# A two-layer transformer on one core: GpSimd's two-input operations in halves, and the order planned anew

## The reference

```python
x = x + attn0(layernorm(x))    # 16 heads of 16, causal softmax, w_qkv, w_out
x = x + ffn0(layernorm(x))     # a = entmax15(layernorm(x @ proj)), 16 experts
#   h = gelu((x @ Win1 + bias) * (a @ C1) @ Wout1.T); out = (h @ Win2 + bias) * (a @ C2) @ Wout2.T
x = x + attn1(layernorm(x))    # low-rank q, k, v; half of each head rotated by cos and sin
x = x + ffn1(layernorm(x))     # relu(x @ Ws1)^2 @ Ws2, and routed experts where the gate is 1
```

## Time and profile before

| | |
|---|---|
| Median of 3 runs | 2663.76 us (2661.55 to 2675.57) |
| The profiled execution | 2670.14 us, span 2667.7 us |
| TensorE | busy 2407.9 us, 90% |
| VectorE | busy 2035.3 us, 76% |
| ScalarE | busy 1869.8 us, 70% |
| GpSimd | busy 1034.1 us, 39% |
| Mean granted TensorE clock | 0.956 |

### The profile page before, as it was taken

The page is one execution under the profiler, slowest core; times in us unless marked ns, Lnnn a source line. Parts: engine busy times, 40 slices in busy tenths (PEclk is TensorE's granted clock), DMA queues, the critical chain, the costliest instruction groups (busy, mean ns, idle before and its releaser), DMA issues.

```text
span 2667.7 us, 68317 instructions
## 1 busy us (share of the span) xinstructions
PE 2407.9 (90%) x24861; PEld 829.7 (31%) x24861; DVE 2035.3 (76%) x5616; ACT 1869.8 (70%) x3804; POOL 1034.1 (39%) x1710
## 2 busy tenths in 40 slices
PE   6889799999999998999989899999999999889784
PEld 3323232333323332333322333233323333233222
DVE  4884688867978688886977869977787958785772
ACT  3578477787668777787667777787677767667472
POOL 2323452344524363253522545334542535253221
PEclk8899799999999999999999999999999999999797
DMA  6211232223222243122321233212332132121211
GB/s 198 78 50 51 82 94 62 83 79 115 88 71 73 68 129 100 58 79 78 113 84 50 70 95 121 72 61 93 109 108 64 62 93 91 47 88 40 85 60 62
DMA packets 192539, 220.40 MB, mean 83 GB/s; under 512 B 36912, under 2 KB 143824, under 8 KB 192208
## 3 DMA queue, kind: packets, MB, share of 16 engines
q1 hardware_dynamic: 192208, 215.97, 26.2%
HBM read 113.07 MB, written 101.71 MB: 81 GB/s over the span
## 4 chain that ended last, share of the span: by engine, by line
PE 65%; DVE 17%; ACT 6%; issue 4%; DMA 4%; POOL 1%; SPq 1%; ACTq 0%; DVEq 0%; POOLq 0%
PE ps L1227 26%; PE ps L1348 16%; PE ps L1290 8%; PE ps L1329 8%; DVE mx L1888 6%; ACT probs L1624 4%; DVE ps L1885 3%; PE ps L1234 2%; PE ps L1304 1%; DMA stk_k<-k 1%; PE ps L1315 1%; DVE st L1852 1%; DVE x L1902 1%; ACT xn L1576 1%; PE ps L1388 1%
## 5 line engine op out<-in xcount | busy, mean ns | idle before, releaser
L1624 ACT ACTIVATE probs<-ps 128x512 f32<-128x512 f32 (+2 forms) x2560 | 1248.3, 559 | 457.4 <-PE ps L1329 449.9
L1888 DVE TENSOR_REDUCE mx<-ps 128x1 f32<-128x512 f32 (+2 forms) x1536 | 897.0, 639 | 193.1 <-PE ps L1290 107.2
L1885 DVE CUSTOM_DVE_ANT_0 ps<-ps,mask_b 128x512 f32<-128x512 f32 (+1 forms) x1024 | 613.4, 652 | 198.6 <-PE ps L1290 194.8
L1785 POOL TENSOR_SCALAR_AFFINE_SELECT probs<-probs 128x256 f32<-128x256 f32 (+1 forms) x768 | 369.4, 485 | 917.7 <-ACT probs L1624 915.8
L1348 PE MATMUL ps<-probs,vaug 128*17 128x512 f32 (+3 forms) x6144 | 615.6, 510 | 8.5 <-POOL probs L1785 3.3
L1290 PE MATMUL ps<-stk_k,stk_q 48*128 48x512 f16 (+3 forms) x3072 | 457.6, 337 | 97.2 <-DMA stk_k<-k 27.9
L1329 PE MATMUL ps<-stk_q,stk_k 50*128 50x512 f16 (+3 forms) x3072 | 455.1, 333 | 71.9 <-DVE mx L1888 28.5
L1329 PEld LDWEIGHTS ps<-stk_q,stk_k 50*128 50x128 f16 x3072 | 137.2, 94 | 520.9 <-issue 370.9
L1290 PEld LDWEIGHTS ps<-stk_k,stk_q 48*128 48x128 f16 x3072 | 140.4, 94 | 474.5 <-issue 339.0
L1227 PE MATMUL ps<-turned,wqkv 128*32 128x512 f32 x2048 | 268.3, 607 | 8.1 <-ACT turned L1563 2.7
L1348 PEld LDWEIGHTS ps<-probs,vaug 128*17 128x17 f32 x6144 | 142.7, 98 | 301.2 <-issue 212.3
(11 more groups left out here) (165 smaller groups left out, 2388.9 us busy)
## 6 DMA issues: line engine op xcount, KB each, us to landing
o<-oT SPq DMA_DIRECT2D x128, 256.0 KB, 2.4
stk_q<-q SPq DMA_DIRECT2D x256, 96.0 KB, 2.4
stk_k<-k SPq DMA_DIRECT2D x128, 192.0 KB, 3.6
q<-parts SPq DMA_DIRECT2D x64, 256.0 KB, 2.1
k<-parts SPq DMA_DIRECT2D x64, 256.0 KB, 2.1
yT<-o SPq DMA_DIRECT2D x64, 256.0 KB
inverse<-inverse_sums SPq DMA_DIRECT2D x64, 256.0 KB
stk_k<-k SPq DMA_DIRECT2D x128, 96.0 KB, 2.4
```

The costliest lines, as they stand in the source:

```text
L1624: act.activation(probs[:, step % PBUF, heads, cols], src, ACT.Exp, scale=exponent[l])\
L1785: pool.affine_select(out=diag, in_=diag, compare_op=ALU.is_ge, fill=0.0, base=0, pattern=[[0, k], [1, P]], channel_multiplier=-1).then_inc ...
L1885: dve.tensor_tensor_reduce(tile, tile, mask_b[:, BANK - width:BANK], 1.0, LOWEST, ALU.add, ALU.max, most)\
L1888: dve.tensor_reduce(most, tile.rearrange("q (k w) -> q k w", k=k), AX.X, ALU.max)\
```

## The change

GpSimd's 384 operations of 512 columns with two inputs are each issued as two of 256 columns, by a helper; only the second half moves the semaphore. In the planner, `port_time` adds up to 0.35 us for each two-input operation of a VectorE item (`TWO_INPUTS`), no more than GpSimd's planned work reaches beyond; steps of the entmax wait while GpSimd is planned ahead by more than the new weight `quiet`; and all 27 rules have other values. `TIMES` is unchanged. The program has the same items.

```diff
+HALF_BANK = BANK // 2
+TWO_INPUTS = {"logit": 3, "ent": {1: 2, 2: 0, 3: 2, 4: 4, 5: 7, 6: 3}, "gate": 4, "stat": 2, "ao": 1, "fo": 1}
+PORT = 0.35
+    def port_time(self, item, time):
+        two = TWO_INPUTS.get(item[0], 0)
+        if item[0] == "ent":
+            two = two[item[3]]
+        return min(max(0.0, self.busy["POOL"] - max(self.busy["DVE"], time)), two * PORT)
+
+    def quiet_time(self, step, rule):
+        return self.busy["POOL"] - rule.quiet if step[0] and step[0][0][0] == "ent" else 0.0
...
             for engine, length in rest:
+                if engine == "DVE":
+                    length += self.port_time(item, time)
...
-    (1.04, 0.13, 3.59, 3.17, 6.66, 9, 2, 3, 5.27, 7.42, 3, 1.01, 11.27, 1.36, 5, 4),
+    (2, 0.6, 2.94, 3.4, 7.19, 6.96, 4, 3.29, 5.16, 8, 2.1, 0.58, 8.39, 0.93, 5, 4, 6),
...
-                if step and not takes_time(step) and plan.ready[n] <= plan.pe:
+                if step and not takes_time(step) and max(plan.ready[n], plan.quiet_time(step, rule)) <= plan.pe:
...
+            def in_halves(out, one, two, op):
+                for half in range(2):
+                    cols = slice(HALF_BANK * half, HALF_BANK * (half + 1))
+                    ins = pool.tensor_tensor(out[:, cols], one[:, cols], two[:, cols], op)
+                return ins
...
-                pool.tensor_tensor(q, q, cos[:, BANK * key[2]:BANK * (key[2] + 1)], ALU.mult).then_inc(cos_ready, 1)
+                in_halves(q, q, cos[:, BANK * key[2]:BANK * (key[2] + 1)], ALU.mult).then_inc(cos_ready, 1)
...
-                pool.tensor_tensor(y, y, inverse[:], ALU.mult).then_inc(y_ready, 1)
+                in_halves(y, y, inverse, ALU.mult).then_inc(y_ready, 1)
```

More of the change, by code:

```diff
@@ L568, in score_work @@
     return sum(2 * (packed(dict(score_parts(i))[p]) * dict(score_parts(i))[p] / 1000 + 0.12) for _, _, i, _, p in score_items(u))
-Rule = namedtuple("Rule", "feed_dve feed_act fed fed_st st s late due pair chain stay pace lead spread ahead_dve ahead_act")
+Rule = namedtuple("Rule", "feed_dve feed_act fed fed_st st s late due pair chain stay pace lead spread ahead_dve ahead_act quiet")
 RULES = [Rule(*values) for values in (
[27 rows of a table removed]
[27 rows of a table added]
 )]
@@ L671, in program_order @@
             if time is not None and not takes_time(plan.head(n)):
-                choices.append((time, 9, "wait", ()))
+                choices.append((max(time, plan.quiet_time(plan.head(n), rule)), 9, "wait", ()))
             elif time is not None:
@@ L1774, in part2 @@
                 pool.wait_ge(part0_ready, PART0[key] + 1)
-                pool.tensor_tensor(parts[:, o % PRING, 1], qf[o % QRING], parts[:, o % PRING, 0], ALU.subtract)\
-                    .then_inc(parts_ready, 1)
+                in_halves(parts[:, o % PRING, 1], qf[o % QRING], parts[:, o % PRING, 0], ALU.subtract).then_inc(parts_ready, 1)
             def causal(u, j, h):
@@ L1789, in rotate @@
                 o, r, w = PROJ["qk", *key], ROPE["rot", *key], key[4]
-                pool.tensor_tensor(qs[w], qs[w], sin[:, BANK * key[2]:BANK * (key[2] + 1)], ALU.mult).then_inc(sin_ready, 1)
+                in_halves(qs[w], qs[w], sin[:, BANK * key[2]:BANK * (key[2] + 1)], ALU.mult).then_inc(sin_ready, 1)
                 pool.wait_ge(cos_ready, r + 1)
                 pool.wait_ge(sin_ready, r + 1)
-                pool.tensor_tensor(qf[o % QRING], qs[w], qf[o % QRING], ALU.add).then_inc(rope_ready, 1)
+                in_halves(qf[o % QRING], qs[w], qf[o % QRING], ALU.add).then_inc(rope_ready, 1)
             def split_max(u):
```

## The result

The changed kernel takes 2686.82 us (median of 4 runs, 2684.17 to 2694.8) and the kernel before 2662.66 us (4 runs, 2658.91 to 2675.57): ratio 1.0084, 95% interval 1.0054 to 1.0115. It is slower by 0.8%. The forecast was 0.8% faster, 2642 us, with a range of 2615 to 2668. The profiled execution took 2687.41 us, 17.3 more than that of before (2670.14); the mean granted clock is 0.956 in both.

A forecast was written before the change was run, and what follows sets the result against it. TensorE, busy 90%, was taken as the bound, so time lay in its work or its 260 us of waits. Terms summed to -21.5 us, giving a median of 2642 us, range 2615 to 2668.

The forecast's parts named there:

- Halves: GpSimd's two-input operations cut in two: +5 us for 73 us more GpSimd work, -9 us for VectorE held more briefly.
- Load behind store: VectorE's statistics waiting for x loads queued behind stores: waits 8.3 us in place of 19.4, worth -9 us.
- The clock term of -3 us: TensorE's halved clock behind the long waits for x loads: partly given back as those waits shrink, -3 us.
- First scores of layer 1: TensorE's 12.69 us hole beside GpSimd's rotation chain: some 4.4 us of scores and values moved in, net -3 us.
- Fewer changes of shape: TensorE switching between row tiles, column strips and whole arrays: 61 fewer changes at 0.09 us each, -5.5 us.
- Sums for the divisions: Less TensorE work between the load of the sums and VectorE's reciprocal in six of 64 places: +3 us.
- I book nothing more for it: The planner's port_time, counting VectorE longer, loosens the order without moving entmax runs from GpSimd's products: no further term.
- the sign: Masks among the releasers of TensorE's matmuls with over 15 us would show the forecast wrong.
- The holes only move: Rival, chance 0.22: the planner's durations open new TensorE holes of 2 to 5 us, worth 15 us; 2657 us.
- GpSimd becomes the one that is late: Rival, chance 0.09: 60% of GpSimd's added 73 us comes out at TensorE, +44 in place of +5; 2681 us.
- The halves don't let VectorE in: Rival, chance 0.05: VectorE is held for both halves, 1.43 us, costing 4 us where 9 were won; 2655 us.
- the waits give back more: Rival, chance 0.20: shorter holds give -18 in place of -9 and TensorE's clock some 10 us more; 2623 us.

The follow-up runs named there:

- the padded kernel: Order before, operations whole, a one-column GpSimd product put ahead of each of the 384 two-input operations: 2672.23 us, 1.0012 of the kernel before.
- e11: Planner of before, whole operations, weight stay (reluctance to change shape) plus 0.3 in all rules: 2719.65 us, 1.0214 of the kernel before.
- the experiments with short tiles: Half the columns of exponentials, maxima or both left out, in order before and new order: new order slower by 20.2, 21.1 and 1.1 us.

## Why the prediction was wrong, step by step

*Halves: right in mechanism, near in size with some luck.* A half takes 731 ns in place of 1278 ns for the whole (734 forecast). Summed one by one, GpSimd's instructions are 73.8 us longer in the kernel after, which is the forecast's 73; its busy time grew by 54.6 us only, because rows that follow each other overlap. So a second half adds 2 x 731 - 1278 = 184 ns by the durations and some 142 ns by busy time. The cost was +3 us for +5, the relief about -10 us for -9. But two errors meet in that -9. The forecast let the holds fall by 22 us and 0.4 of it reach TensorE; between the padded kernel and the halves they fell by 15.6 us, and some 0.6 of it reached the time. In the kernel after, the holds are 147 with 48.6 us (107 with 60.2 before by the same reckoning, 38 forecast), and the product of the earlier trace rows reaches 823 ns at most.

The Trainium skill (SBUF — State Buffer, Who interferes with whom) has GpSimd wait too where VectorE issues first, for which the forecast reckoned 25 us. The trace agrees with the rule, and the size is small. In the kernel after, a mask of 256 columns that began 0.07 us behind a running sum of VectorE took 0.56 us where the median is 0.41:

```profile
1495.14 0.42 DVE L1969 TENSOR_TENSOR_SCAN cum<-going,cum 128x128 f32<-128x128 f32 x1
1495.21 0.56 POOL L1804 TENSOR_SCALAR_AFFINE_SELECT probs<-probs 128x256 f32<-128x256 f32 x1
```

No such case added more. All 94 instructions of GpSimd that began in the middle of a VectorE operation with two inputs in SBUF are together 1 us longer than the medians of their kinds.

*Load behind store: right.* 8.96 us of waits for 8.3 (single ones up to 1.3 us off), and TensorE's idle time behind them fell by 9.6 us for 9. The clock term of -3 us came out the other way in the kernel after: the mean is 0.956 before and after, but 15.8 us more of TensorE's work fell in stretches at the lower level. At 598 ns against 1022 this costs 6 to 7 us (an estimate from these two durations and one profiled execution each). In the new order alone the median of the mean clocks was 0.960 against 0.957 for before, so it is not settled whether the order causes this.

*First scores of layer 1: half right.* The work did move into the hole, but it waits there: 12.69 us became 12.13 in five pieces. That is 0.6 us for the forecast's 3. The forecast counted the values as work that fills the hole and not the masks that they stand behind, which stand in GpSimd's order among the very rotation that makes the hole.

*Fewer changes of shape: not seen.* -5.5 us rests on a price taken from one pair of neighbours. No run changed only the number of changes; e11 shows that it does not decide.

*Sums for the divisions (+3 us): not seen.* VectorE's waits for these loads did not grow but fell, from 33.8 us in 13 places to 21.7 in 12. What this is worth at TensorE no run tested.

*"I book nothing more for it": the step that failed.* The forecast wrote this of `port_time`, whose looser order it looked at beside the entmax alone; and its sum has no other term for what a new order of 6216 items does away from the places looked at. It added up long idle stretches and put the short ones at nothing. The order alone had terms of -9 - 3 - 5.5 - 3 + 3 = -17.5 us; it measured +15.5, which is 33 us off. The profiled executions show 27 of the 33, as that of before (2670.14) lies 3.9 us above the median of 2666.22 and that of the new order alone (2679.33) 2.4 under its own. What they show:

| TensorE, us | before | new order alone | after |
|---|---|---|---|
| idle stretches over 2 us | 87.0 | 50.1 | 60.3 |
| idle stretches of 0.15 to 2 us | 154.2 (319 of them) | 186.6 (391) | 179.5 (384) |
| busy with the same matmuls | 2407.9 | 2417.9 | 2424.0 |

The order took 37 us out of the long stretches, far more than the forecast asked of it. It put 32 us into short ones, 3 us into gaps shorter still and 10 us into busy time. Of the short ones, those that end with an exponential grew from 37.6 to 51.1 us, with a maximum from 56.1 to 64.4, with a mask from 3.3 to 8.3. This fits the experiments with short tiles: the waits are behind both engines that empty the score tiles. Why the same matmuls are busy for longer is open.

GpSimd's masks were judged by the trace of before alone: 40.5 us of waiting weights, hardly any of it at the matmuls. In the new kernel the same group is

```profile
who waited for it (us, times):
  PEld ps L1362: 60.4, 121
  PE ps L1362: 15.4, 14
```

and 15.4 us is just over the 15 that the forecast named as a sign that it would be wrong. As 6.2 of them stand in the old hole, the sign came true partly by a change of label.

*The rivals.* "The holes only move" was right that the order gives back what it wins, and wrong in how and in price: 15 us, for new holes of 2 to 5 us. The new waits are under 2 us and many, which nobody sees in a list of the longest. "GpSimd becomes the one that is late" came near the measured time (2681) for a wrong reason: it blamed the halves' 73 us, and these cost 3 in the order before. Of the 12.1 us that masks release more, 7.6 came with the order, 6.1 of them in the hole; 4.5 came when the halves were put on top, where no gain of theirs is seen (1.0060 without, 1.0084 with, the intervals overlap). "The halves don't let VectorE in" is refuted by the longest product, 1321 ns padded and 703 with halves. Nothing supports "the waits give back more" in the time: the long waits did shrink by more than forecast, but the clock did not help and the short waits grew.

*Open.* That the new order loses is shown; what in it loses is read from the profile. No run moved only the values, or only their masks. Nor is it settled what in an order makes the short waits: bunches are a correlation, and that both engines must be slack is shown for this one pair of orders. And whether halves bring nothing on the new order or a little can't be told from these intervals.

The version that beats both kernels is the order before with halves: 0.9974 (0.9963 to 0.9985).

## What to carry to other kernels

Take a change to an operation and a new plan of the order apart before judging either: here one was worth -7 us and the other +16, and the sum hid the gain. When a plan is new, don't sum up only the places that look better; compare the short waits with the long ones, and line by line what each matmul waits for. Look where a wait stood before you call it new, for it may only have changed its line. And ask what stands ahead of the inputs on the engine that makes them, because thousands of moves that nobody looked at weigh more than five that somebody did. Here an order did not survive a change of one part of its plan: four of the five other orders that were tried, each with one weight, the rules or `port_time` changed, lost 2.1 to 2.6%; the fifth was nearly the order before.

## What the runs showed of the hardware

A VectorE operation with two inputs that was held by GpSimd gets in between two GpSimd instructions that follow each other without a wait: with halves the longest of a group fell from 1321 to 703 ns. A GpSimd product of one column takes 191 ns (384 of them, 73.3 us), but 384 of them ahead of other work added 53 us to its busy time (1034.1 to 1087.3 us), as much as cutting the 384 operations in two did (1086.9). The hold goes both ways: a mask that began while VectorE's running sum had 0.35 us to go took 0.56 us for 0.41. Halving the columns of every maximum, in the order before, took 565 us off VectorE's busy time (2035.3 to 1470.6) and 2.2% off the time. Halving those of every exponential took 454 us off ScalarE's (1869.8 to 1416.2) and only 0.7% off the time. A busy time says little of what shortening it is worth.
